# Eight pair sums per band go from VectorE to accumulating transfers begun by GpSimd, and a grouped convolution is placed in nine steps of TensorE's order

## Chip, cores and metric

The kernel runs on one core of a Trainium2 chip. The metric is the device time of one execution in microseconds (us), as the median of several executions. The engines are called PE (TensorE), DVE (VectorE), ACT (ScalarE), POOL (GpSimd) and SP (SyncE).

## What is computed

The input is x of shape (8, 128, 128, 128): images, channels, rows, columns, in float32. There are two stages. The first, `mix_tokens`, is windowed attention and a two-layer perceptron; the change doesn't touch it. The second, `convolve`, is this, cut from the reference:

```
enh  = conv3x3_depthwise(conv1x1(x))                       # 128 channels
h    = conv3x3(x, groups=16)                               # 16 channels
attn = conv1x1(h1 * h2) * gamma + conv1x1(x)               # 16 coefficients for each pixel; h1, h2 are the halves of h
attk = einsum('bpn,nm->bpm', attn, selfw)                  # for each pixel: 64 groups x 2 outputs x (2 channels x 9 taps)
y    = sum over channel of the pair and tap of attk * shifted enh, plus attn @ selfb
out  = y * ga1 + enh + x
```

## The kernel before

An image is cut into 8 bands of 16 rows, so there are 64 bands. Every engine runs its own instruction list through `pipelined(engine, bands, 4, step)`: one step handles up to four bands at once, `l, m, n, o` (the newest first), each in another part of the work. In a step the heavy part is that of band `n`: 36 products, numbered q = 0 to 35. q stands for chunk j = q // 9 (4 rows, 512 pixels, one PSUM bank) and tap t = q % 9.

For product q, PE makes the kernels of both channel halves with two matmuls (`basis_kernels`, L826, into `ps_k`, two buffers of two banks). DVE multiplies them with the shifted `enh` (`product`, L1055) into `products`, a ring of 12 buffers of 128 x 1024. PE then adds a product up by transposing it into `ps_t` (`add_term`, L842, eight 128 x 128 transposes that accumulate). After the last term of a chunk come four transposes of `enh_x`, which is enh + x (L850), ACT copies the sum to SBUF (L946), and PE transposes it back and adds the bias term (`back`, L857 and L859).

To spare PE a third of the terms, twelve pairs (q, q + 1) are summed before they reach it. Eight pairs, `VECTOR_MERGES`, are summed by DVE (L1062) and four, `POOL_MERGES` = 6, 15, 24, 33, by POOL (L765). That leaves 24 terms.

The order on each engine is written out by hand:

- PE goes through 36 slots a step. In slot q it issues the kernels of product q + 2, which wait until product q is made; then the terms whose `TERM_SLOT` is q or, for band `o`, q + 36; then `back`; then pairs of grouped-convolution matmuls (`group_taps`, L809, 18 pairs a band) whose entry in `CONV_SLOTS` is this slot, or this slot + 36; then `coefficients` (L816, slot 22) and a pointwise block (L795, `PW_SLOTS`). A matmul of the grouped convolution fills 32 of 128 columns of PE; a pair of entries covers two chunks in two column groups.
- POOL goes through 16 places a step: 16 additions of a depthwise tap that ACT has scaled (`add_tap`, L753; eight on 10 rows, eight on 8 rows, at places 0 to 7 and 8 to 15), `add_input` (L758, place 1.5, which waits for the last chunk sum of the band before), and the four merges at places 2.6, 5.5, 10.5 and 13.95. All are executed in the order of their places.
- DVE goes through q = 0 to 35: the product, then the merge of q - 2 if there is one. It also does its part of `add_input` (L1046), `h_prod` (L1079) and `att_lo` (L1082).
- SP issues all transfers of the stage: bands in, chunks out, the swap of channel pairs in `enh`, and the coefficient rows.

Buffer reuse is guarded in `buffer_free`: product q may overwrite buffer q % 12 once the term or the merge that read it is done.

Of the kernel before, what the change touches and what calls it, by code (L numbers as in the profile page):

```python
# [44 lines left out]
TAPS = 9  # L45
# [4 lines left out]
HALVES = ((0, 10), (10, 18))  # L50


VECTOR_MERGES = (0, 3, 10, 12, 18, 21, 27, 30)
POOL_MERGES = (6, 15, 24, 33)

OPS = [op for q in range(Q) for op in [("product", q)] + [("merge", q - 2)] * (q - 2 in VECTOR_MERGES)]
OP_COUNT = {op: i + 1 for i, op in enumerate(OPS)}
PARTNERS = {q + 1 for q in VECTOR_MERGES + POOL_MERGES}

TERMS = [q for q in range(Q) if q not in PARTNERS]  # L60
VECTOR_TERMS = [q for q in TERMS if q not in POOL_MERGES]
TERM_SLOT = dict(zip(TERMS, (3, 4, 8, 9, 13, 11, 11, 16, 18, 19, 21, 19, 22, 24, 25, 26, 30, 28, 31, 33, 35, 36, 40, 37)))
FIRST_TERM = [min((TERM_SLOT[q], q) for q in TERMS if q // TAPS == j)[1] for j in range(CHUNKS)]
LAST_TERM = [max((TERM_SLOT[q], q) for q in TERMS if q // TAPS == j)[1] for j in range(CHUNKS)]
TERM_COUNT = {q: i + 1 for i, q in enumerate(sorted(VECTOR_TERMS, key=lambda q: (TERM_SLOT[q], q)))}

BACK_SLOTS = [15, 23, 32, 42]

POOL_PLACES = 2 * (TAPS - 1)
ADD_INPUT_PLACE = 1.5  # L70
# [8 lines left out]

H_PROD_SLOT = 21  # L80
ATT_HIGH, ATT_LOW = 23.8, 25
CONV_SLOTS = [28, 28, 29, 31, 34, 34, 37, 37, 38, 39, 42, 43, 43, 46, 46, 48, 48, 50]
COEFFICIENT_SLOT = 22
PW_SLOTS = [13, 17, 20, 24, 27]

# [445 lines left out]
def convolve(nc, x2, out, w_pw, b_pw, w_dw, b_dw, w_g, b_g, w_att, b_att, w_211, b_211, gamma, ga1, selfb, selfw):  # L531
# [4 lines left out]
    with ExitStack() as ctx:  # L536
# [64 lines left out]
        tap_ready, dw_done, enh_ready, enh_x_ready = sem("tap_ready"), sem("dw_done"), sem("enh_ready"), [sem(f"enh_x_ready{i}") for i in range(2)]  # L601
        swapped = [[sem(f"swapped{p}_{h}") for h in range(2)] for p in range(2)]
        k_done, product_ready, term_done = sem("k_done"), sem("product_ready"), sem("term_done")
        pool_merged, pool_term_done = sem("pool_merged"), sem("pool_term_done")
        sum_done, sumT_ready, back_done, out_ready = sem("sum_done"), sem("sumT_ready"), sem("back_done"), sem("out_ready")
        stored = [sem(f"chunk_stored{j}") for j in range(CHUNKS)]
# [18 lines left out]
        with nc.Block() as block:  # L625
# [87 lines left out]
            def _(pool):  # L713
# [46 lines left out]

                def merge(n, index):
                    q = POOL_MERGES[index]
                    pool.wait_ge(product_ready, len(OPS) * n + OP_COUNT["product", q + 1])
                    lead = products[:, q % PRODUCTS, :, :]
                    nc.gpsimd.tensor_tensor(lead, lead, products[:, (q + 1) % PRODUCTS, :, :], ALU.add).then_inc(pool_merged, 1)  # L765


                ORDER = ([(t - 1, add_tap, 1, (0, t)) for t in range(1, TAPS)] +
                         [(TAPS - 1 + t - 1, add_tap, 1, (1, t)) for t in range(1, TAPS)] +
                         [(ADD_INPUT_PLACE, add_input, 2, ())] +  # L770
                         [(place, merge, 2, (i,)) for i, place in enumerate(POOL_MERGE_PLACES)])

                def step(items, p):
                    for place, action, part, args in sorted(ORDER, key=lambda entry: entry[0] % POOL_PLACES):
                        k = part + (place >= POOL_PLACES)
                        if items[k] is not None:
                            if action is merge:
# [7 lines left out]
            def _(pe):  # L785
# [32 lines left out]
                def basis_kernels(n, p, q):  # L818

                    j, t = divmod(q, TAPS)  # L820
                    if q >= 2:
                        pe.wait_ge(product_ready, len(OPS) * n + OP_COUNT["product", q - 2])
                    else:
                        at_least(pe, product_ready, len(OPS) * (n - 1) + OP_COUNT["product", q + Q - 2])
                    for s in range(2):
                        mm = nc.tensor.matmul(ps_k[q % 2][:, BANK * s:BANK * (s + 1)], basis[:, 2 * t + s, :], att[p][:, j, :],  # L826
                                              start=True, stop=True)
                    mm.then_inc(k_done, 1)

                def add_term(n, q):  # L830

                    j = q // TAPS
                    if q in POOL_MERGES:
                        pe.wait_ge(pool_merged, len(POOL_MERGES) * n + POOL_MERGES.index(q) + 1)
                    else:
                        kind = "merge" if q in VECTOR_MERGES else "product"
                        pe.wait_ge(product_ready, len(OPS) * n + OP_COUNT[kind, q])
# [62 lines left out]
            def _(act):  # L900
# [53 lines left out]
                def tap_product(m, p, h, t):  # L954

                    dy, dx = divmod(t, 3)
                    lo, hi = HALVES[h]
                    src = e0[p][:, lo + dy:hi + dy, dx:dx + W]
                    if t == 0:
                        if h == 0:  # L960
                            act.wait_ge(e0_ready, PW_CHUNKS * m + PW_CHUNKS)

                            at_least(act, enh_x_ready[0], m - 1)
                            for swap in swapped[p]:
                                at_least(act, swap, rounds(m, p, 32))
                            at_least(act, product_ready, len(OPS) * (m - 1))
# [28 lines left out]
            def _(dve):  # L995
# [35 lines left out]
                def buffer_free(n, q):  # L1031

                    before, at = (n, q - PRODUCTS) if q >= PRODUCTS else (n - 1, q - PRODUCTS + Q)
                    if at in POOL_MERGES:
                        at_least(dve, pool_term_done, len(POOL_MERGES) * before + POOL_MERGES.index(at) + 1)
                    elif at in VECTOR_TERMS:
                        at_least(dve, term_done, len(VECTOR_TERMS) * before + TERM_COUNT[at])
                    elif at - 1 in POOL_MERGES:
                        at_least(dve, pool_merged, len(POOL_MERGES) * before + POOL_MERGES.index(at - 1) + 1)
                    else:  # L1040
                        at_least(dve, product_ready, len(OPS) * before + OP_COUNT["merge", at - 1])

                def add_input(n, p):
                    dve.wait_ge(dw_done, 2 * (TAPS - 1) * (n + 1))
# [11 lines left out]
                                            ps_k[q % 2][:, :].rearrange("c (s h w) -> c s h w", s=2, w=W),  # L1056
                                            enh[p][:, :, r:r + CHUNK_ROWS, dx:dx + W], ALU.mult).then_inc(product_ready, 1)

                def merge(n, q):
                    dve.wait_ge(product_ready, len(OPS) * n + OP_COUNT["product", q + 1])  # L1060
                    lead = products[:, q % PRODUCTS, :, :]
                    nc.vector.tensor_tensor(lead, lead, products[:, (q + 1) % PRODUCTS, :, :], ALU.add).then_inc(product_ready, 1)  # L1062

                def step(items, p):
                    l, m, n, o = items
                    for q in range(Q):
                        if m is not None and q == H_PROD_SLOT:
                            dve.wait_ge(moved, 64 * (m + 1))
                        if n is not None:
# [47 lines left out]
```

## Time and profile before

| | |
|---|---|
| Median of 3 executions | 6324.29 us (6320.84 to 6329.96) |
| The profiled execution | 6323.67 us |
| Its span, first to last instruction | 6321.9 us |
| Mean granted clock of TensorE | 0.993 |
| Busy over the span | PE 94%, PE weight loads 65%, DVE 87%, ACT 55%, POOL 73% |

The busy times are sums over the whole span, and the two stages have different limits, so the second stage, which begins near 2130 us, is looked at in windows of its own. Matmuls are pipelined and their ends are modelled: a busy PE is not PE at its peak, and the distance between the starts of two matmuls says more than their durations.

### The profile page before, as it was taken

To read this page: it belongs to the slowest core of one execution; us is meant where nothing else is said; L and a number is where in the kernel's file an instruction comes from. 1 tells how busy PE (TensorE), PEld (TensorE's weight loads), DVE (VectorE), ACT (ScalarE), POOL (GpSimd) and SP (SyncE) were. 2 spreads that over 40 slices of the span, in tenths; PEclk is the share of its full clock that TensorE was granted. 3 is DMA by queue.
4 is the path that set the end of the run, shared out by engine and by line. 5 is a ranking of instruction groups with operands and counts; after the bars stand their busy time and mean duration, and the time that the engine had idled before them with its cause. 6 is when DMAs were issued, how large, how long until landed. Compare 5 with 4: busy or idle time off the path is not lost.

```text
span 6321.9 us, 117871 instructions
## 1 busy us (share of the span) xinstructions
PE 5944.1 (94%) x39944; PEld 4123.6 (65%) x39944; DVE 5481.4 (87%) x5380; ACT 3446.0 (55%) x4288; POOL 4621.9 (73%) x1893
## 2 busy tenths in 40 slices
PE   8999999999999699999999999999999999999998
PEld 6777777777776366666666666666666666666666
DVE  6777777777776799999999999999999999999999
ACT  6777777777776444444444444444444444444443
POOL 4444444444444698888888888888888888888886
PEclk9999999999999799999999999999999999999999
DMA  2222222222221222211222112222221212112221
GB/s 80 66 66 66 66 66 66 66 66 66 66 66 53 58 67 64 67 60 62 65 63 66 61 60 65 63 66 64 64 62 62 65 62 67 60 61 65 63 66 43
DMA packets 303448, 403.66 MB, mean 64 GB/s; under 512 B 38192, under 2 KB 202736, under 8 KB 303344
## 3 DMA queue, kind: packets, MB, share of 16 engines
q1 hardware_dynamic: 303008, 402.45, 20.3%
q10 hardware_dynamic: 400, 0.69, 0.1%
q8 instruction: 24, 0.39, 0.0%
q14 instruction: 16, 0.13, 0.0%
HBM read 152.26 MB, written 136.31 MB: 46 GB/s over the span
## 4 chain that ended last, share of the span: by engine, by line
PE 49%; issue 9%; DVE 9%; SPq 0%; DVEq 0%; DMA 0%; ACT 0%
PE ps_k L826 16%; PE ps_t L842 16%; PE ps_m L809 9%; DVE products L1055 5%; PE ps_p L795 3%; PE ps_t L859 2%; DVE products L1062 2%; PE ps_t L857 1%; PE ps_t L850 1%; PE ps_m L816 1%; DVE h_prod L1079 1%; DVE products L1021 1%; SPq L631 0%; DVEq L1053 0%; SPq L681 0%
## 5 line engine op out<-in xcount | busy, mean ns | idle before, releaser
L753 POOL TENSOR_TENSOR enh<-enh,tap 128x1280 f32<-128x1280 f32 (+1 forms) x1024 | 2831.9, 2766 | 165.6 <-ACT tap L972 116.7
L1055 DVE TENSOR_TENSOR products<-ps_k,enh 128x1024 f32<-128x1024 f32 x2304 | 2750.6, 1217 | 213.6 <-PE ps_k L826 187.5
L826 PE MATMUL ps_k<-att,basis 128*128 128x512 f32 x4608 | 1764.0, 464 | 197.3 <-DVE products L1055 192.1
L842 PE MATMUL ps_t<-ident,products 128*128 128x128 f32 x12288 | 1568.6, 272 | 0.0
L842 PEld LDWEIGHTS ps_t<-ident,products 128*128 128x128 f32 x12288 | 1426.5, 141 | 184.5
L826 PEld LDWEIGHTS ps_k<-att,basis 128*128 128x128 f32 x4608 | 715.9, 189 | 1089.0 <-DVE products L1055 630.6
L257 POOL TENSOR_TENSOR hidden_lo<-hidden,hidden_hi 128x1024 fp32r<-128x1024 f32 x256 | 651.9, 2565 | 894.2 <-DVE hidden_hi L452 894.2
L972 ACT ACTIVATE tap<-e,dw 128x1280 f32<-128x1280 f32 (+1 forms) x1024 | 1245.8, 1248 | 8.2 <-POOL enh L753 8.2
L1062 DVE TENSOR_TENSOR products<-products 128x1024 f32<-128x1024 f32 x512 | 1110.4, 2169 | 0.0
L765 POOL TENSOR_TENSOR products<-products 128x1024 f32<-128x1024 f32 x256 | 614.8, 2401 | 409.9 <-DVE products L1055 409.9
L809 PE MATMUL ps_m<-xin,gT 128*32 128x512 f32 x4608 | 814.2, 609 | 2.8 <-DVE bias_att L1012 2.8
L946 ACT ACTIVATE summedT<-ps_t 128x512 f32<-128x512 f32 x256 | 153.2, 599 | 1060.3 <-PE ps_t L850 1060.2
L433 ACT ACTIVATE hidden<-ring,bias 128x512 f32<-128x512 f32 x512 | 352.0, 689 | 389.1 <-PE ring L285 387.6
L262 POOL TENSOR_TENSOR x_lo<-xt,x_hi 128x512 fp32r<-128x512 f32 x256 | 321.0, 1277 | 183.6 <-DVE x_hi L469 183.6
L282 PE MATMUL ring<-x_hi,w_hi 128*128 128x512 f32 x1024 | 426.9, 417 | 6.6 <-DVE x_hi L469 2.6
L285 PE MATMUL ring<-x_lo,w_hi 128*128 128x512 f32 x1024 | 432.5, 422 | 0.4 <-POOL x_lo L262 0.4
L920 ACT ACTIVATE e<-ps_p,bias_pw 128x512 f32<-128x512 f32 (+1 forms) x320 | 192.7, 602 | 412.6 <-PE ps_p L795 412.6
L283 PE MATMUL ring<-x_hi,w_lo 128*128 128x512 f32 x1024 | 406.7, 397 | 0.0
L795 PE MATMUL ps_p<-xin,pwT 128*128 128x512 f32 x640 | 334.6, 605 | 14.1 <-DMA xin<-layer_out 8.5
L456 DVE TENSOR_REDUCE row_sum<-expd 128x8 f32<-128x512 f32 x128 | 87.8, 686 | 295.3 <-ACT expd L409 295.3
L951 ACT ACTIVATE out_sb<-ps_t 128x512 f32<-128x512 f32 x256 | 152.7, 596 | 325.3 <-PE ps_t L859 325.3
L285 PEld LDWEIGHTS ring<-x_lo,w_hi 128*128 128x128 f32 x1024 | 193.0, 188 | 136.9 <-DVE x_lo L489 100.5
(106 smaller groups left out, 7209.7 us busy)
## 6 DMA issues: line engine op xcount, KB each, us to landing
xt<-in_x SPq DMA_DIRECT2D x128, 512.0 KB, 4.1
layer_out<-xo SPq DMA_DIRECT2D x128, 512.0 KB, 2.9
out<-out_sb SPq DMA_DIRECT2D x256, 256.0 KB, 2.0
xin<-layer_out SPq DMA_DIRECT2D x63, 896.0 KB, 5.6
enh<-enh SPq DMA_DIRECT2D x128, 325.0 KB, 2.7
enh<-enh SPq DMA_DIRECT2D x128, 260.0 KB, 2.4
xin<-layer_out SPq DMA_DIRECT2D x63, 384.0 KB, 6.2
att<-att_hi SPq DMA_DIRECT2D x512, 32.0 KB, 1.9
```

The source lines that it names most:

```text
L257: nc.gpsimd.tensor_tensor(hidden_lo[:, h, :, :], hidden[:, h, :, :], hidden_hi[:, h, :, :].bitcast(FP32), ALU.subtract).then_inc(hidden_lo ...
L282: nc.tensor.matmul(out, w_hi[:, w, :], hi, start=start, stop=False)
L285: return nc.tensor.matmul(out, w_hi[:, w, :], lo, start=False, stop=stop)
L753: nc.gpsimd.tensor_tensor(own, own, tap_sb[add % TAP_BUFFERS][:, 0:hi - lo, :], ALU.add).then_inc(dw_done, 1)
L765: nc.gpsimd.tensor_tensor(lead, lead, products[:, (q + 1) % PRODUCTS, :, :], ALU.add).then_inc(pool_merged, 1)
L795: nc.tensor.matmul(ps_p[:, :], pwT[:, :], xin[p][:, CHUNK_ROWS * c:CHUNK_ROWS * (c + 1), 1:W + 1], start=True, stop=True).then_inc(pw_done, 1)
L809: mm = nc.tensor.matmul(ps_m[32 * j:32 * j + 32, :], gT[:, t, :], xin[p][:, r:r + CHUNK_ROWS, dx:dx + W], start=(t == 0), stop=(t == TAPS ...
L826: mm = nc.tensor.matmul(ps_k[q % 2][:, BANK * s:BANK * (s + 1)], basis[:, 2 * t + s, :], att[p][:, j, :], start=True, stop=True)
L842: mm = nc.tensor.matmul(ps_t[j % 2][:, C * r:C * (r + 1)], products[:, q % PRODUCTS, s, C * r:C * (r + 1)], ident[:, :], is_transpose=True ...
L972: nc.scalar.activation(tap_sb[add % TAP_BUFFERS][:, 0:hi - lo, :], src, ACT.Copy, scale=dw[:, t:t + 1]).then_inc(tap_ready, 1)
L1055: nc.vector.tensor_tensor(products[:, q % PRODUCTS, :, :].rearrange("c s (h w) -> c s h w", w=W), ps_k[q % 2][:, :].rearrange("c (s h w) - ...
L1062: nc.vector.tensor_tensor(lead, lead, products[:, (q + 1) % PRODUCTS, :, :], ALU.add).then_inc(product_ready, 1)
```

## The change

DVE no longer sums pairs. For each of the eight pairs (now 0, 3, 9, 12, 18, 21, 27, 30; 9 in the place of 10), POOL waits for product q + 1 and begins a transfer of 128 x 1024 float32 from SBUF to SBUF that adds the partner's buffer to the lead's. PE waits for the landing, on a semaphore of its own for each pair, before it takes the term. The transfers get places in POOL's order by a formula: (q + 2.5) / 36 x 16, which is 1.11, 2.44, 5.11, 6.44, 9.11, 10.44, 13.11 and 14.44. `TERM_SLOT` is written anew, so that such a term comes 5.5 slots behind the place; the slots of the four POOL merges' terms stay (13, 21, 30, 40). `CONV_SLOTS` holds each slot twice, nine different slots in place of twelve. The counters of `product_ready` now count products alone (Q = 36 a band).

```diff
-VECTOR_MERGES = (0, 3, 10, 12, 18, 21, 27, 30)
+DMA_MERGES = (0, 3, 9, 12, 18, 21, 27, 30)
 POOL_MERGES = (6, 15, 24, 33)
-OPS = [op for q in range(Q) for op in [("product", q)] + [("merge", q - 2)] * (q - 2 in VECTOR_MERGES)]
-TERM_SLOT = dict(zip(TERMS, (3, 4, 8, 9, 13, 11, 11, 16, 18, 19, 21, 19, 22, 24, 25, 26, 30, 28, 31, 33, 35, 36, 40, 37)))
+TERM_SLOT = {0: 8, 2: 4, 3: 11, 5: 9, 6: 13, 8: 10,
+             9: 17, 11: 14, 12: 20, 14: 16, 15: 21, 17: 19,
+             18: 26, 20: 23, 21: 29, 23: 25, 24: 30, 26: 28,
+             27: 35, 29: 32, 30: 38, 32: 34, 33: 40, 35: 37}
...
+DMA_MERGE_PLACES = {q: (q + 2.5) / Q * 2 * (TAPS - 1) for q in DMA_MERGES}
...
-CONV_SLOTS = [28, 28, 29, 31, 34, 34, 37, 37, 38, 39, 42, 43, 43, 46, 46, 48, 48, 50]
+CONV_SLOTS = [28, 28, 31, 31, 33, 33, 36, 36, 39, 39, 42, 42, 44, 44, 47, 47, 50, 50]
...
+        dma_merged = {q: sem(f"dma_merged{q}") for q in DMA_MERGES}
...
+                def merge_by_dma(n, q):
+                    pool.wait_ge(product_ready, Q * n + q + 2)
+                    pool.sem_inc(dma_merge_begun, 1)
+                    nc.gpsimd.dma_start(products[:, q % PRODUCTS, :, :], products[:, (q + 1) % PRODUCTS, :, :],
+                                        accum_op=ALU.add).then_inc(dma_merged[q], 16)
...
-                         [(place, merge, 2, (i,)) for i, place in enumerate(POOL_MERGE_PLACES)])
+                         [(place, merge, 2, (i,)) for i, place in enumerate(POOL_MERGE_PLACES)] +
+                         [(place, merge_by_dma, 2, (q,)) for q, place in DMA_MERGE_PLACES.items()])
...
+                    elif q in DMA_MERGES:
+                        pe.wait_ge(dma_merged[q], 16 * n + 16)
...
-                def merge(n, q):
-                    dve.wait_ge(product_ready, len(OPS) * n + OP_COUNT["product", q + 1])
-                    lead = products[:, q % PRODUCTS, :, :]
-                    nc.vector.tensor_tensor(lead, lead, products[:, (q + 1) % PRODUCTS, :, :], ALU.add).then_inc(product_ready, 1)
...
-                            if ("merge", q - 2) in OPS:
-                                merge(n, q - 2)
```

## Rows read from the trace of the kernel before

**Rows 1.** The page, parts 1 and 2: busy time, and DVE in 40 slices.

```profile
PE 5944.1 (94%) x39944; PEld 4123.6 (65%) x39944; DVE 5481.4 (87%) x5380; ACT 3446.0 (55%) x4288; POOL 4621.9 (73%) x1893
...
DVE  6777777777776799999999999999999999999999
```

**Rows 2.** Window: length, busy us of PE, PEld, DVE, ACT, POOL, clock, DMA share, GB/s.

```profile
3000.00:6000.00 3000.00, 2865.91 (x17586) 1888.00 (x17583) 2851.91 (x2154) 1439.82 (x1696) 2610.22 (x962) 1.00 0.20 63
```

**Rows 3.** The instruction att_lo, 3000 to 6000 us: count, durations, first and last start.

```profile
L1082 DVE SCALAR_TENSOR_TENSOR att_lo<-ps_m,bias_att,att_hi x46: 731/735/737, 3038.8 to 5985.5; 128x512 fp32r<-128x512 f32 x46
```

**Rows 4.** Waits, 3000 to 6000 us: us in total, times, longest us.

```profile
PE ps_k L826 <- DVE products L1055: 134.1, 183, 1.7
```

**Rows 5.** Groups by line, 3000 to 6000 us: count, busy us, mean ns, idle before.

```profile
L753 POOL TENSOR_TENSOR enh<-enh,tap 128x1280 f32<-128x1280 f32 (+1 forms) x733 | 2030.5, 2770 | 91.3 <-ACT tap L972 59.0
L1055 DVE TENSOR_TENSOR products<-ps_k,enh 128x1024 f32<-128x1024 f32 x1649 | 1970.1, 1217 | 147.4 <-PE ps_k L826 129.7
...
L1062 DVE TENSOR_TENSOR products<-products 128x1024 f32<-128x1024 f32 x367 | 804.2, 2191 | 0.0
...
L765 POOL TENSOR_TENSOR products<-products 128x1024 f32<-128x1024 f32 x183 | 438.9, 2399 | 271.3 <-DVE products L1055 271.3
...
L758 POOL TENSOR_TENSOR enh_x<-enh,xin 128x1536 f32<-128x1536 f32 x46 | 155.2, 3374 | 22.9 <-PE ps_t L850 22.9
```

**Rows 6.** Timeline of DVE and POOL in one band: start us, us.

```profile
4032.35 1.22 DVE L1062 TENSOR_TENSOR products<-products 128x1024 f32<-128x1024 f32 x1
...
4040.99 1.23 DVE L1055 TENSOR_TENSOR products<-ps_k,enh 128x1024 f32<-128x1024 f32 x1 [0.21 <-PE ps_k L826]
...
4074.63 3.61 DVE L1062 TENSOR_TENSOR products<-products 128x1024 f32<-128x1024 f32 x1
...
4023.46 4.47 POOL L753 TENSOR_TENSOR enh<-enh,tap 128x1024 f32<-128x1024 f32 x2
...
4036.80 2.40 POOL L765 TENSOR_TENSOR products<-products 128x1024 f32<-128x1024 f32 x1 [5.73 <-DVE products L1055]
...
4071.68 5.48 POOL L753 TENSOR_TENSOR enh<-enh,tap 128x1280 f32<-128x1280 f32 x2
```

**Rows 7.** Timeline of PE in the same band: start us, us.

```profile
4021.41 1.02 PE L795 MATMUL ps_p<-xin,pwT 128*128 128x512 f32 x2
...
4022.73 1.04 PE L842 MATMUL ps_t<-ident,products 128*128 128x128 f32 x8
4023.52 0.72 PE L826 MATMUL ps_k<-att,basis 128*128 128x512 f32 x2
4024.08 1.03 PE L842 MATMUL ps_t<-ident,products 128*128 128x128 f32 x8
...
4027.72 1.07 PE L809 MATMUL ps_m<-xin,gT 128*32 128x512 f32 x8
4028.72 0.72 PE L826 MATMUL ps_k<-att,basis 128*128 128x512 f32 x2
4029.37 1.05 PE L809 MATMUL ps_m<-xin,gT 128*32 128x512 f32 x4
4030.36 0.73 PE L826 MATMUL ps_k<-att,basis 128*128 128x512 f32 x2
...
4040.15 0.71 PE L826 MATMUL ps_k<-att,basis 128*128 128x512 f32 x2
```

**Rows 8.** Timeline of SP, the issues of eight small transfers.

```profile
4019.88 5.04 SPq L681 DMA_DIRECT2D att<-att_hi  x8
```

**Rows 9.** DMA issues, page part 6: count, KB each, us to landing.

```profile
xt<-in_x SPq DMA_DIRECT2D x128, 512.0 KB, 4.1
layer_out<-xo SPq DMA_DIRECT2D x128, 512.0 KB, 2.9
...
xin<-layer_out SPq DMA_DIRECT2D x63, 896.0 KB, 5.6
```

More of the change, by code:

```diff
@@ L50 @@
 HALVES = ((0, 10), (10, 18))
-VECTOR_MERGES = (0, 3, 10, 12, 18, 21, 27, 30)
+DMA_MERGES = (0, 3, 9, 12, 18, 21, 27, 30)
 POOL_MERGES = (6, 15, 24, 33)
-OPS = [op for q in range(Q) for op in [("product", q)] + [("merge", q - 2)] * (q - 2 in VECTOR_MERGES)]
-OP_COUNT = {op: i + 1 for i, op in enumerate(OPS)}
-PARTNERS = {q + 1 for q in VECTOR_MERGES + POOL_MERGES}
+MERGES = DMA_MERGES + POOL_MERGES
+PARTNERS = {q + 1 for q in MERGES}
 TERMS = [q for q in range(Q) if q not in PARTNERS]
-VECTOR_TERMS = [q for q in TERMS if q not in POOL_MERGES]
-TERM_SLOT = dict(zip(TERMS, (3, 4, 8, 9, 13, 11, 11, 16, 18, 19, 21, 19, 22, 24, 25, 26, 30, 28, 31, 33, 35, 36, 40, 37)))
+LONE_TERMS = [q for q in TERMS if q not in POOL_MERGES]
+TERM_SLOT = {0: 8, 2: 4, 3: 11, 5: 9, 6: 13, 8: 10,
[3 rows of a table added]
 FIRST_TERM = [min((TERM_SLOT[q], q) for q in TERMS if q // TAPS == j)[1] for j in range(CHUNKS)]
 LAST_TERM = [max((TERM_SLOT[q], q) for q in TERMS if q // TAPS == j)[1] for j in range(CHUNKS)]
-TERM_COUNT = {q: i + 1 for i, q in enumerate(sorted(VECTOR_TERMS, key=lambda q: (TERM_SLOT[q], q)))}
+TERM_COUNT = {q: i + 1 for i, q in enumerate(sorted(LONE_TERMS, key=lambda q: (TERM_SLOT[q], q)))}
 BACK_SLOTS = [15, 23, 32, 42]
+DMA_MERGE_PLACES = {q: (q + 2.5) / Q * 2 * (TAPS - 1) for q in DMA_MERGES}
 POOL_PLACES = 2 * (TAPS - 1)
@@ L603, in convolve @@
         k_done, product_ready, term_done = sem("k_done"), sem("product_ready"), sem("term_done")
+        dma_merge_begun = sem("dma_merge_begun")
+        dma_merged = {q: sem(f"dma_merged{q}") for q in DMA_MERGES}
         pool_merged, pool_term_done = sem("pool_merged"), sem("pool_term_done")
@@ L762, in merge @@
                     q = POOL_MERGES[index]
-                    pool.wait_ge(product_ready, len(OPS) * n + OP_COUNT["product", q + 1])
+                    pool.wait_ge(product_ready, Q * n + q + 2)
                     lead = products[:, q % PRODUCTS, :, :]
                     nc.gpsimd.tensor_tensor(lead, lead, products[:, (q + 1) % PRODUCTS, :, :], ALU.add).then_inc(pool_merged, 1)
+                def merge_by_dma(n, q):
+                    pool.wait_ge(product_ready, Q * n + q + 2)
+                    pool.sem_inc(dma_merge_begun, 1)
+                    nc.gpsimd.dma_start(products[:, q % PRODUCTS, :, :], products[:, (q + 1) % PRODUCTS, :, :],
+                                        accum_op=ALU.add).then_inc(dma_merged[q], 16)
                 ORDER = ([(t - 1, add_tap, 1, (0, t)) for t in range(1, TAPS)] +
@@ L776, in step @@
                         if items[k] is not None:
-                            if action is merge:
+                            if action in (merge, merge_by_dma):
                                 action(items[k], *args)
@@ L821, in basis_kernels @@
                     if q >= 2:
-                        pe.wait_ge(product_ready, len(OPS) * n + OP_COUNT["product", q - 2])
+                        pe.wait_ge(product_ready, Q * n + q - 1)
                     else:
-                        at_least(pe, product_ready, len(OPS) * (n - 1) + OP_COUNT["product", q + Q - 2])
+                        at_least(pe, product_ready, Q * n + q - 1)
                     for s in range(2):
@@ L834, in add_term @@
                         pe.wait_ge(pool_merged, len(POOL_MERGES) * n + POOL_MERGES.index(q) + 1)
-                    else:
-                        kind = "merge" if q in VECTOR_MERGES else "product"
-                        pe.wait_ge(product_ready, len(OPS) * n + OP_COUNT[kind, q])
+                    elif q in DMA_MERGES:
+                        pe.wait_ge(dma_merged[q], 16 * n + 16)
+                    else:
+                        pe.wait_ge(product_ready, Q * n + q + 1)
                     if q == FIRST_TERM[j]:
@@ L965, in tap_product @@
                                 at_least(act, swap, rounds(m, p, 32))
-                            at_least(act, product_ready, len(OPS) * (m - 1))
+                            at_least(act, product_ready, Q * (m - 1))
                         nc.scalar.activation(enh[p][:, 0, lo:hi, 1:W + 1], src, ACT.Identity, bias=bias_dw[:, 0:1],
@@ L1035, in buffer_free @@
                         at_least(dve, pool_term_done, len(POOL_MERGES) * before + POOL_MERGES.index(at) + 1)
-                    elif at in VECTOR_TERMS:
-                        at_least(dve, term_done, len(VECTOR_TERMS) * before + TERM_COUNT[at])
+                    elif at in LONE_TERMS:
+                        at_least(dve, term_done, len(LONE_TERMS) * before + TERM_COUNT[at])
                     elif at - 1 in POOL_MERGES:
@@ L1040, in buffer_free @@
                     else:
-                        at_least(dve, product_ready, len(OPS) * before + OP_COUNT["merge", at - 1])
+                        at_least(dve, dma_merged[at - 1], 16 * before + 16)
                 def add_input(n, p):
```

## The prediction

> **What bounds the kernel now.** I begin with engine shares and slices [rows 1]. No engine is full over the whole span, and VectorE (DVE) and GpSimd (POOL) step up where the second stage begins, so the stage is read alone. From 3000 to 6000 us [rows 2] TensorE (PE) is busy 2866 of 3000 us (96%), DVE 2852 (95%), POOL 2610 (87%), at clock 1.00, which is the 2.4 GHz level; so no time is lost to the clock. The step of one band is read from an instruction that comes once in it: att_lo, 46 times between starts at 3038.8 and 5985.5 us [rows 3], so 2946.7 / 45 = 65.5 us a band. There are 64 bands: a microsecond saved in each is 64 us of the span.
>
> Who makes the band 65.5 us long? By the waits [rows 4] PE stands idle for DVE's products 134 us in 45.8 bands, 2.9 us a band; DVE for PE 130 us, 2.8 [rows 5]. Neither is clearly the limit: products and kernels alternate over two PSUM buffers, PE is slightly the longer, and where DVE adds a pair PE runs dry. POOL has room: its merges wait for products 271 us [rows 5], 5.9 us a band, nearly all at one of them (5.73 at 4036.80 [rows 6]).
>
> **What goes from DVE.** The eight L1062 sums take 804 us in 45.8 bands [rows 5], 17.5 us a band. Alone such a sum takes 1.22 us (at 4032.35, POOL idle until 4036.80); beside POOL's adds 3.61 us (at 4074.63) [rows 6]. DVE's rest is 62.3 - 17.5 = 45 us (62.3 is 95% of 65.5). It stops being a limit. POOL's adds have the same quarrel: ten rows take 2.70 us in the pair at 4071.68 (next start 2.78 later), eight rows 2.20 in the pair at 4023.46 (4.47 less the pause of 0.08, halved) [rows 6], against the mean of 2.77 for both sizes [rows 5]. POOL's own work becomes 8 x 2.78 + 8 x 2.28 + 4 x 2.37 (L765) + 3.35 (L758) = 53.3 us, down from 57.
>
> The Trainium skill ("SBUF — State Buffer", Who interferes with whom) states that a VectorE instruction with two SBUF inputs and a GpSimd one that reads SBUF take turns on a shared port, and one with a single SBUF input does not. By that rule, the trace agrees: L1062 varies threefold, while L1055, which reads PSUM and SBUF, is steady at 1.22 us.
>
> **What goes from PE.** The grouped convolution goes from 12 places to 9. A place with four column groups (4027.72) takes 1.00 us until the next ps_k, one with two groups (4029.37) 0.99 [rows 7]: filling a half-empty place is free. A ps_k pair ahead of a place takes 0.65 (from 4028.72) instead of 0.56 (from 4023.52), so each place removed gives 1.1 us, 3.3 a band. The 24 terms stay. PE's floor is 65.5 - 2.9 - 3.3 = 59.3 us. Were that all, the gain would be 6.2 us a band, 400 us.
>
> **What comes to POOL, and its order.** Eight transfers of 512 KB a band. No row shows an accumulating transfer or one begun by GpSimd, so two prices are bounded: D, the time POOL is held by one, and L, from there to landing. For D the nearest row is SP's pace, 8 issues in 5.04 us, 0.63 each [rows 8]; above, the POOL add of the same shape, 2.40 [rows 5]. An accumulating row names three places instead of two, so I take 1.5 times SP's, D = 0.95. For L: transfers of 512 KB land 2.9 and 4.1 us after issue, 896 KB 5.6 us [rows 9]. An accumulating one moves three streams of 512 KB (two read, one written) instead of two, so 1.5 times 2.9 to 1.5 times 4.1, 4.4 to 6.2 us; I take L = 5.2. Its ends are 2.9 (the second read is free) and 8.2 (twice 4.1).
>
> In the place of DVE's sums, each transfer has 5.5 of 36 slots, 5.5 x 65.5 / 36 = 10 us, between its place and its term. But POOL executes in order, and two of them stand behind a POOL merge that waits for a later product. merge 15 (place 5.5) waits for product 16; behind it tap 7, then transfer 12 (place 6.44), whose term PE wants in slot 20. merge 33 (13.95) waits for product 34; behind it tap 7 of the lower half, then transfer 30 (14.44), wanted in slot 38, which is slot 2 of the next step. PE is in order as well: everything behind that term, the kernels for the coming products too, stands.
>
> PE from slot 20's term until the kernels of product 34 (slot 32), costed by [rows 7]: 8 terms each with a ps_k pair at 1.34 (4022.73 to 4024.08), 4 pairs alone at 0.55, two places 2.2, three pointwise blocks at 0.77 (4021.41 to 4022.73, less a pair), the coefficients, of the same shape, 0.8, one back 0.6 (half a term and one matmul), two enh_x sums 0.8 (each half a term): 19.6 us. From slot 2 to the kernels of product 16: the same terms and pairs 12.9, four places 4.4, one pointwise 0.8, back 0.6, enh_x 0.8: 19.5. After each the product still needs 1.6 us (DVE starts at 4040.99 [rows 6], 0.84 after its pair at 4040.15, of which 0.55 is counted; 1.2 for itself; 0.1 to reach POOL). The cycle through both is 19.6 + 19.5 + 2 x 1.6 + merges 2 x 2.4 + taps 2.8 + 2.3 + 2(D + L) = 52.2 + 2(D + L).
>
> The half after product 34 is longer than that, as POOL comes late to merge 15. add_input (L758) waits for the last sum of the band before, which PE makes in slot 4, behind the term of transfer 30. From product 34: merge and tap 4.65, D + L, PE's slots 2 to 4 up to that sum (terms 30 and 33 at 0.8, two ps_k pairs at 0.55, one place 1.1, enh_x 0.4) 4.2; then POOL's add_input 3.35, tap 2.8, transfer D, merge 6 2.4, three taps 8.3, transfer D: 16.8 + 2D; merge 15 and tap 5.2, D + L, and 19.6 + 1.6 to the next product 34. Sum: 52.1 + 4D + 2L. With my values 52.1 + 3.8 + 10.4 = 66.3 us, and the first cycle is 52.2 + 12.3 = 64.5.
>
> So the band takes the longest of PE's 59.3, POOL's 53.3 + 8 x 0.95 = 60.9, 64.5 and 66.3 us: 66.3, 0.8 more than now: 64 x 0.8 = 51 us. The sum is made against the profiled execution, 6323.7 us (span 6321.9, 1.8 around it), within 0.6 of the median of 6324.3. Forecast: 6324 + 51 = 6375 us. PE waits more than before though it does less; the saved 17.5 us on DVE turn into idle time. The stages before are untouched.
>
> **Rivals.**
>
> 1. Forecast (chance 0.49): the two late transfers set the band, slower; 65.7 to 70.7 us (D = 1.4 and L = 6.5: 52.1 + 5.6 + 13.0), that is 6337 to 6657 us.
> 2. The same cycle, but transfers land fast (0.36), the other side. It needs 4D + 2L below 13.4; with D = 0.95, L below 4.8. For it speaks the 2.9 us row; against it that this row is a plain copy. At L = 3.5, the middle of the two rows, 52.1 + 3.8 + 7.0 = 62.9 us, 2.6 less: 6158 us. At both lower ends (0.63, 2.9) 60.4 us: 5998.
> 3. GpSimd as the bound (0.10): if D is near the 2.4 of the add it replaces, POOL has 53.3 + 19.2 = 72.5 and the cycle 52.1 + 9.6 + 10.4 = 72.1 us: 72.5, 6772. It decides over the present band from D = 1.5 upward by POOL's sum alone. For it: POOL is the fullest after the change; against it: the rows show issues at 0.63.
> 4. The transfers are hidden (0.05): if POOL does not stand where I put it, PE's 59.3 or POOL's 60.9 decides: 64 x 4.6 less, 6030 us.
>
> The Trainium skill ("DMA: Bandwidth & Descriptors", Anatomy of one DMA) gives a GpSimd-begun transfer 2.0 us plus bytes over 436 GB/s. By that rule an estimate for 512 KB is 3.2 us from issue to landing, on the side of rival 2; no run here shows it for an accumulating one. The same page (Specifications) puts the first byte at about 1 us for transfers begun by GpSimd against 0.6 from SP; the trace agrees with SP's side only as far as its issue pace of 0.63 goes.
>
> **From this to the numbers.** No change, within 0.2% (about 13 us, what a measurement of this kernel can tell), is the strip between cases 1 and 2 (4D + 2L within 0.2 of 13.4): 0.09, of it 0.05 from case 1 and 0.04 from rival 2. Faster: 0.32 of rival 2 and 0.05 of rival 4, 0.37. Slower: 0.44 of case 1 and 0.10 of rival 3, 0.54. The range reaches from the point of rival 2, 6158, to the end of case 1, 6657 us; beyond each end lies about 1 in 10. Case 1's own range is 6337 to 6657.
>
> **What would show it.** In the profile after: L1062 gone, DVE near 68% (45 of 66.3) of the stage; L753 steady at 2.7 and 2.2; POOL's transfers with their D; in the waits, PE's terms idle for the transfers twice a band (slots 20 and 2), not eight times; POOL idle at add_input for PE's enh_x sum. Wrong would be: transfers that land within 4 us (then faster), one that holds POOL for over 1.5 us, waits at all eight terms (then transfers share the DMA engines badly: they are busy 20% now [rows 2], and 64 x 8 x 512 KB are 268 MB on top), or a band set by PE with no idle time.

## The result, and the profile after

The changed kernel takes 6977.7 us (median of 4, 6967.6 to 6991.0); the kernel before took 6325.9 us in the same comparison. The ratio is 1.103, 95% interval 1.101 to 1.106: slower by 10%, outside the range of 6158 to 6657 us. The direction is the forecast one, the size is not: 51 us were forecast and 652 came. The profiled execution took 6967.6 us, with a span of 6965.8 us.

The page, its parts 1, 2 and 3, against [rows 1]:

```profile
PE 5921.9 (85%) x39944; PEld 4206.8 (60%) x39944; DVE 5002.3 (72%) x4868; ACT 3429.3 (49%) x4288; POOL 4725.3 (68%) x2405
...
PEclk9999999999988998998999999899999899999989
DMA  2111111112123444444444444444444444444444
...
q0 software_dynamic: 73728, 268.47, 20.3%
```

The first stage, up to about 2130 us, is as before. In the second every compute engine is less busy than before, the DMA engines are more than twice as busy (the transfers are queue q0, 268 MB), and the granted clock, which was full, is not. The window from 3500 to 6500 us answers to [rows 2], the occurrences of att_lo to [rows 3] (count, durations in ns, first and last start):

```profile
3500.00:6500.00 3000.00, 2465.11 (x15222) 1682.67 (x15220) 2172.15 (x1547) 1235.54 (x1464) 2324.56 (x1151) 0.92 0.47 110
```

```profile
L1087 DVE SCALAR_TENSOR_TENSOR att_lo<-ps_m,bias_att,att_hi x39: 741/742/743, 3559.7 to 6433.0; 128x512 fp32r<-128x512 f32 x39
```

A band takes (6433.0 - 3559.7) / 38 = 75.6 us instead of 65.5. 64 bands of 10.1 us more are 646 us, nearly the whole loss of 652. Who waits, from 3500 to 6500 us (us in total, times, longest), against [rows 4]:

```profile
PE ps_k L837 <- DVE products L1067: 374.4, 40, 9.4
...
PE ps_t L854 <- DMA products<-products: 156.6, 118, 1.6
```

In 39.7 bands PE waits for landings 118 times, three a band, 3.9 us. Two a band were foreseen. But it also waits once a band, 40 times, for 9.4 us for a product of DVE, an engine that was to be two thirds busy (68%; it is 72%). The groups on the page name the reason (count, busy us, mean ns):

```profile
L1058 DVE TENSOR_TENSOR enh_x<-enh,xin 128x512 f32<-128x512 f32 x64 | 615.7, 9621 | 0.0
...
L775 POOL DMA_DIRECT2D products<-products x512 | 472.4, 923 | 7.8 <-DVE products L1067 7.8
```

L1058 is DVE's part of `add_input`, 128 x 512 with both operands in SBUF. The change doesn't touch it. It takes 9.6 us in the mean. The timeline of one band (start us, us; first DVE, then POOL, then PE):

```profile
4499.26 1.22 DVE L1067 TENSOR_TENSOR products<-ps_k,enh 128x1024 f32<-128x1024 f32 x1 [1.34 <-PE ps_k L837]
4500.40 9.83 DVE L1058 TENSOR_TENSOR enh_x<-enh,xin 128x512 f32<-128x512 f32 x1
```

```profile
4497.36 0.86 POOL L775 DMA_DIRECT2D products<-products  x1
4497.97 3.23 POOL L762 TENSOR_TENSOR enh_x<-enh,xin 128x1536 f32<-128x1536 f32 x1
4500.87 2.97 POOL L757 TENSOR_TENSOR enh<-enh,tap 128x1280 f32<-128x1280 f32 x1
```

```profile
4503.50 1.17 POOL L775 DMA_DIRECT2D products<-products  x1
4504.11 2.94 POOL L769 TENSOR_TENSOR products<-products 128x1024 f32<-128x1024 f32 x1
4506.42 9.12 POOL L757 TENSOR_TENSOR enh<-enh,tap 128x1280 f32<-128x1280 f32 x3
```

```profile
4501.30 0.74 PE L837 MATMUL ps_k<-att,basis 128*128 128x512 f32 x2
4511.42 1.22 PE L837 MATMUL ps_k<-att,basis 128*128 128x512 f32 x2 [9.38 <-DVE products L1067]
4512.44 1.91 PE L854 MATMUL ps_t<-ident,products 128*128 128x128 f32 x8
```

L1058 starts while POOL does its own part of `add_input` and ends in the middle of the last POOL row, behind the first of its three taps. POOL goes through add_input, tap, transfer, merge, tap without a gap; each starts before the one ahead of it ends (4500.87 against 4497.97 + 3.23 = 4501.20). Behind the first of the three taps comes the first pause, 0.07 to 0.08 us as between any two taps, and there DVE gets in. DVE stands until then, and the products with it, and so PE. When PE goes on, its transposes run at half speed: eight take 1.91 us where they took 1.04 [rows 7]. That is the 1.2 GHz level, after 9.4 us in which PE did nothing.

In the kernel before the same instruction stood beside the same two additions of POOL (one DVE row, then two of POOL):

```profile
4053.31 1.15 DVE L1046 TENSOR_TENSOR enh_x<-enh,xin 128x512 f32<-128x512 f32 x1
```

```profile
4050.53 3.38 POOL L758 TENSOR_TENSOR enh_x<-enh,xin 128x1536 f32<-128x1536 f32 x1 [0.49 <-PE ps_t L850]
4053.88 3.16 POOL L753 TENSOR_TENSOR enh<-enh,tap 128x1280 f32<-128x1280 f32 x1
```

There it was let in when POOL's add_input ended at 4053.91, though the tap had begun 0.03 us earlier. In the changed kernel add_input stands behind a transfer; it begins before that one's end and hands an overlap of 0.33 us on.

### The profile page after: what moved, and what is told of

Its sections match the earlier page's. It is cut to its first block, busy times and chain, and to the rows that moved or that the text cites. A ratio compares the mean times of both kernels' runs of the same rounds, so it can differ in the third digit from the quotient of the medians.

```text
span 6965.8 us, 117933 instructions
## 1 busy us (share of the span) xinstructions
PE 5921.9 (85%) x39944; PEld 4206.8 (60%) x39944; DVE 5002.3 (72%) x4868; ACT 3429.3 (49%) x4288; POOL 4725.3 (68%) x2405
## 4 chain that ended last, share of the span: by engine, by line
issue 32%; POOL 19%; PE 8%; DMA 6%; ACT 3%; DVE 1%; POOLq 1%; SPq 1%; ACTq 0%; DVEq 0%
POOL enh L757 13%; DMA products<-products 6%; POOL products L769 4%; PE ps_t L854 4%; POOL products L775 2%; ACT tap L984 2%; PE ps_k L837 2%; PE ps_p L806 1%; PE ps_t L862 1%; DVE products L1033 0%; PE ps_m L820 0%; SPq L635 0%; PE ps_t L871 0%; ACT enh L952 0%; POOLq L754 0%
## 5 line engine op out<-in xcount | busy, mean ns | idle before, releaser
L1067 DVE TENSOR_TENSOR products<-ps_k,enh 128x1024 f32<-128x1024 f32 x2304 | 2794.8, 1223 | 1330.6 <-PE ps_k L837 1291.8
L757 POOL TENSOR_TENSOR enh<-enh,tap 128x1280 f32<-128x1280 f32 (+1 forms) x1024 | 2679.1, 2616 | 260.0 <-ACT tap L984 221.5
L854 PE MATMUL ps_t<-ident,products 128*128 128x128 f32 x12288 | 1678.7, 282 | 257.4 <-DMA products<-products 257.4
L854 PEld LDWEIGHTS ps_t<-ident,products 128*128 128x128 f32 x12288 | 1490.8, 146 | 529.1 <-DMA products<-products 340.5
L837 PEld LDWEIGHTS ps_k<-att,basis 128*128 128x128 f32 x4608 | 763.2, 196 | 1378.2 <-DVE products L1067 857.9
L769 POOL TENSOR_TENSOR products<-products 128x1024 f32<-128x1024 f32 x256 | 679.5, 2654 | 872.2 <-DVE products L1067 872.2
L820 PE MATMUL ps_m<-xin,gT 128*32 128x512 f32 x4608 | 656.7, 645 | 2.7 <-DVE bias_att L1024 2.7
L1058 DVE TENSOR_TENSOR enh_x<-enh,xin 128x512 f32<-128x512 f32 x64 | 615.7, 9621 | 0.0
L775 POOL DMA_DIRECT2D products<-products x512 | 472.4, 923 | 7.8 <-DVE products L1067 7.8
L806 PE MATMUL ps_p<-xin,pwT 128*128 128x512 f32 x640 | 360.2, 647 | 16.2 <-DMA xin<-layer_out 10.5
```

What stands on the lines that cost most here:

```text
L757: nc.gpsimd.tensor_tensor(own, own, tap_sb[add % TAP_BUFFERS][:, 0:hi - lo, :], ALU.add).then_inc(dw_done, 1)
L775: nc.gpsimd.dma_start(products[:, q % PRODUCTS, :, :], products[:, (q + 1) % PRODUCTS, :, :], accum_op=ALU.add).then_inc(dma_merged[q], 16)
L806: nc.tensor.matmul(ps_p[:, :], pwT[:, :], xin[p][:, CHUNK_ROWS * c:CHUNK_ROWS * (c + 1), 1:W + 1], start=True, stop=True).then_inc(pw_done, 1)
L820: mm = nc.tensor.matmul(ps_m[32 * j:32 * j + 32, :], gT[:, t, :], xin[p][:, r:r + CHUNK_ROWS, dx:dx + W], start=(t == 0), stop=(t == TAPS ...
L1058: nc.vector.tensor_tensor(enh_x[:, ADD_SPLIT:ROWS, :], enh[p][:, 0, ADD_SPLIT + 1:ROWS + 1, 1:W + 1], xin[p][:, ADD_SPLIT + 2:ROWS + 2, 1: ...
L1067: nc.vector.tensor_tensor(products[:, q % PRODUCTS, :, :].rearrange("c s (h w) -> c s h w", w=W), ps_k[q % 2][:, :].rearrange("c (s h w) - ...
```

## The experiments

All are compared with the kernel before on the same chip. The period of a band is read from att_lo as above, between 3000 and 6300 us.

### DVE's part of add_input at another moment

```diff
-VECTOR_ADD_SLOT = 8
+VECTOR_ADD_SLOT = 15
```

> The changed kernel with DVE's part of add_input (L1058) moved from slot 8 to slot 15, a moment in which POOL stands idle. Theory A, one blocked DVE instruction makes the loss: L1058 took 9.80 us in the changed kernel against 1.15 before, and PE, which gets no products meanwhile, falls to the lower clock behind it. Then L1058 is under 2 us here and the band falls from 75.6 us by 8.6 for it and about 1 for the clock, to 66 us; the execution is 6968 - 64 x 9.6 = 6350 us, within 60. Theory B, the transfers and POOL's order hold the band by themselves and the blocked instruction lies beside them: L1058 is short as well, but the band stays above 71 us and the time above 6680 us.

Measured: 6922.5 us, ratio 1.095 (1.093 to 1.097). L1058 fell to 1.9 us, as both theories said, but the time hardly moved. Theory B seemed to win. A wait of this kernel, 3500 to 6300 us, shows why that reading is wrong:

```profile
PE ps_p L806 <- DMA xin<-layer_out: 279.7, 37, 8.0
```

A new wait of 7.6 us a band took the place of the old one: SP loads the second part of a coming band's rows only when DVE's `add_input` has read the buffer, and PE's first pointwise block in slot 13 needs them. The experiment moved two things. It decides nothing.

### A pause behind POOL's add_input

```diff
                                             xin[p][:, 2:ADD_SPLIT + 2, 1:W + 1], ALU.add).then_inc(enh_x_ready[0], 1)
+                    pool.wait_ge(enh_x_ready[0], n + 1)
```

> The changed kernel with one added wait on POOL: after its part of add_input it waits for that addition's own semaphore before the next tap, which makes a pause of about 0.08 us as between two taps. L1058 stays in slot 8. Theory P, DVE's instruction with two SBUF inputs gets its turn only where POOL pauses between two instructions: L1058 ends right after POOL's add_input, in 1.3 to 2 us, and the band is as in the run with slot 15, 66 us (6350 us). Rival, something else keeps DVE out from the transfer's issue on (the descriptors being written, or the landing): L1058 stays above 5 us and the time above 6600 us.

Measured: 6505.1 us, ratio 1.028 (1.027 to 1.030). One added wait of POOL gives back 473 us of the 652. Two rows of POOL's timeline, then L1059 (the same instruction as L1058, one line lower) and att_lo from 3000 to 6000 us:

```profile
4477.48 3.20 POOL L762 TENSOR_TENSOR enh_x<-enh,xin 128x1536 f32<-128x1536 f32 x1
4480.91 2.89 POOL L757 TENSOR_TENSOR enh<-enh,tap 128x1280 f32<-128x1280 f32 x1 [0.24 <-POOL enh_x L762]
```

```profile
L1059 DVE TENSOR_TENSOR enh_x<-enh,xin x44: 1286/1334/1367, 3046.4 to 5990.6; 128x512 f32<-128x512 f32 x44
L1088 DVE SCALAR_TENSOR_TENSOR att_lo<-ps_m,bias_att,att_hi x44: 741/742/743, 3013.7 to 5958.0; 128x512 fp32r<-128x512 f32 x44
```

With 0.24 us between the two POOL instructions DVE is let in: 1.33 us. The blocked instruction was the main cause. But the band is 2944.3 / 43 = 68.5 us, not the 66 that were expected. One band of this kernel shows PE's four waits for a landing, the terms of transfers 3, 12, 18 and 30 in this order:

```profile
4491.04 1.97 PE L855 MATMUL ps_t<-ident,products 128*128 128x128 f32 x8 [2.67 <-DMA products<-products]
...
4510.67 1.83 PE L855 MATMUL ps_t<-ident,products 128*128 128x128 f32 x8 [1.58 <-DMA products<-products]
...
4524.05 1.09 PE L855 MATMUL ps_t<-ident,products 128*128 128x128 f32 x8 [1.51 <-DMA products<-products]
...
4544.71 1.09 PE L855 MATMUL ps_t<-ident,products 128*128 128x128 f32 x8 [1.07 <-DMA products<-products]
```

Transfers 12 and 30 are the two that the prediction named. Transfer 18 is begun late, as POOL stands for a tap of ACT ahead of it, and transfer 3 is slow: it is begun 1.9 us behind SP's load of a coming band's rows, which the end of POOL's `add_input` releases, and lands 7.3 us after its issue, where transfers 12 and 30 take 4.5. In order of time, SP's load, transfer 3 and the tap ahead of transfer 18:

```profile
4481.81 1.29 SPq L670 DMA_DIRECT2D xin<-layer_out  x2
4483.74 0.88 POOL L776 DMA_DIRECT2D products<-products  x1
4516.13 2.20 POOL L757 TENSOR_TENSOR enh<-enh,tap 128x1024 f32<-128x1024 f32 x1 [3.86 <-ACT tap L985]
```

### What hands the overlap on: transfer 0, transfer 3, or none

Three kernels leave transfers out; the partners' products are then missing from the sums, and PE takes the lead product alone. With `LEFT_OUT = (0,)`, `(3,)` or all eight:

```diff
-                         [(place, merge_by_dma, 2, (q,)) for q, place in DMA_MERGE_PLACES.items()])
+                         [(place, merge_by_dma, 2, (q,)) for q, place in DMA_MERGE_PLACES.items() if q not in LEFT_OUT])
...
-                    elif q in DMA_MERGES:
+                    elif q in DMA_MERGES and q not in LEFT_OUT:
...
-                    else:
+                    elif at - 1 not in LEFT_OUT:
```

> The changed kernel with transfer 0 alone left out, the one that POOL begins just ahead of its add_input (its partner is missing from the sum). In the changed kernel POOL's instructions overlap by 0.3 us behind a transfer and by 0.6 behind a second one, with no gap in which DVE's L1058 gets in. If the overlap that add_input inherits from transfer 0 is what blocks, L1058 is let in at the end of add_input as in the kernel before, 1.2 to 2 us, and the time is near that with the pause, 6500 us. If any transfer or merge behind it blocks, L1058 stays above 5 us and the time above 6850 us.

> The changed kernel with transfer 3 alone left out, the one that POOL begins while L1058 stands blocked (its partner is missing from the sum). If the overlap inherited from transfer 0 blocks, L1058 is still shut out through add_input, the tap and merge 6, above 7 us. If the transfer that comes while it waits is to blame, L1058 gets in at an earlier boundary, under 5 us.

> The changed kernel with all eight transfers left out: POOL doesn't begin them, PE takes the lead product alone as the term, so the eight partners are missing from the sums. No pause added, L1058 in slot 8. It prices the transfers and tests what blocks DVE. If L1058 is blocked by transfers among POOL's additions, it is back at 1.2 us here; if back-to-back additions on POOL are enough, it stays above 5 us. If it is short, the band is PE's own: my floor was 59.3 us, so 6324 - 64 x 6.2 = 5930 us; if above 62 us a band (6100), the floor in the prediction was too low.

Without transfer 0: 6579.0 us (one execution), DVE's `add_input`, L1059 here, at 1.05. Without transfer 3: 6923.4 us (one execution), still shut out. POOL and DVE in the kernel without transfer 0, then DVE's `add_input` in the one without transfer 3:

```profile
4320.72 2.94 POOL L763 TENSOR_TENSOR enh_x<-enh,xin 128x1536 f32<-128x1536 f32 x1 [0.54 <-PE ps_t L863]
4323.61 3.16 POOL L758 TENSOR_TENSOR enh<-enh,tap 128x1280 f32<-128x1280 f32 x1
```

```profile
4323.16 1.05 DVE L1059 TENSOR_TENSOR enh_x<-enh,xin 128x512 f32<-128x512 f32 x1
```

```profile
L1059 DVE TENSOR_TENSOR enh_x<-enh,xin x40: 8852/8928/8982, 3053.6 to 5975.8; 128x512 f32<-128x512 f32 x40
```

It is the transfer in front of `add_input` that does it, not the one that is begun while DVE stands. Here the overlap at 4323.61 is 0.05 us, as before the change, and DVE gets in; transfer 3 behind it, at 4326.71, doesn't shut it out. (That transfer again lands late, 7.2 us after its issue, with SP's load begun at 4324.72 and transfer 0 not there at all.) Why this kernel takes 74 us more than the one with the pause was not tested by a run; from 3000 to 6000 us PE stands 6.9 us a band for landings instead of 6.5, and its granted clock is 0.96 instead of 0.98.

With no transfers: 5935.0 us, ratio 0.938 (0.937 to 0.940), and a band of (5863.4 - 3015.4) / 48 = 59.3 us:

```profile
L1088 DVE SCALAR_TENSOR_TENSOR att_lo<-ps_m,bias_att,att_hi x49: 737/743/744, 3015.4 to 5863.4; 128x512 fp32r<-128x512 f32 x49
```

This is the floor of PE that the prediction had worked out, 59.3 us.

### The order of transfer 0 and add_input

```diff
-DMA_MERGE_PLACES = {q: (q + 2.5) / Q * 2 * (TAPS - 1) for q in DMA_MERGES}
+DMA_MERGE_PLACES = {q: (q + 2.5) / Q * 2 * (TAPS - 1) for q in DMA_MERGES} | {0: 1.6}
```

> The changed kernel with one step of POOL's order changed: add_input stands ahead of transfer 0 and not behind it (place of transfer 0: 1.6). No pause is added, all eight transfers are made. Theory, add_input begun before the transfer in front of it is over carries an overlap of 0.3 us with it that shuts DVE out: add_input is now begun behind a tap, with an overlap of 0.04 us, L1058 is let in at its end, 1.0 to 1.4 us, and the time is near that of the pause, 6450 to 6600 us. Rival, the pause helped for another reason and any transfer near L1058 shuts it out: L1058 above 5 us, the time above 6850 us.

Measured: 6677.6 us, ratio 1.057 (1.055 to 1.058). POOL, then DVE:

```profile
4497.43 2.94 POOL L762 TENSOR_TENSOR enh_x<-enh,xin 128x1536 f32<-128x1536 f32 x1 [0.54 <-PE ps_t L862]
4500.30 0.86 POOL L775 DMA_DIRECT2D products<-products  x1
```

```profile
4499.87 1.05 DVE L1058 TENSOR_TENSOR enh_x<-enh,xin 128x512 f32<-128x512 f32 x1
```

L1058 takes 1.05 us with all eight transfers made, one of them right behind `add_input`. The theory of the overlap holds. The time is 78 us above the range that I expected: PE stands 8.2 us a band for landings (346.3 us from 3000 to 6000 us) instead of 6.5 with the pause, and its granted clock is 0.96 instead of 0.98. Transfers 0 and 3 are now begun 3.3 us apart, and SP's load of a coming band's rows is issued between them, at 4501.44; transfer 3 lands 10.2 us after its issue. PE's waits for landings, then the time from issue to landing (min/median/max, all transfers, 3500 to 6200 us):

```profile
PE ps_t L854 <- DMA products<-products: 346.3, 170, 4.2
```

```profile
DMA to landing us min/median/max: 4.5/5.6/10.3
```

### The transfers behind merges

On slot 15 (first kernel), and then on the kernel with the pause, transfers 12 and 30 go ahead of merges 15 and 33:

```diff
-DMA_MERGE_PLACES = {q: (q + 2.5) / Q * 2 * (TAPS - 1) for q in DMA_MERGES}
+DMA_MERGE_PLACES = {q: (q + 2.5) / Q * 2 * (TAPS - 1) for q in DMA_MERGES} | {12: 5.4, 30: 13.9}
```

> As the run with slot 15, and transfers 12 and 30 begun ahead of POOL's merges 15 and 33 (places 5.4 and 13.9) instead of behind merge and tap. Prediction's mechanism: each late transfer costs its merge and tap, about 5 us of delay, at PE's slots 20 and 2; with them early those two waits of PE for a landing vanish and the band comes down to PE's floor or POOL's sum, 60 to 62 us: 5.0 us less than with slot 15 alone, about 6030 to 6080 us. Rival: the waits for landings are covered by others (ACT's taps, POOL's arrears), and the gain on the run with slot 15 is under 1 us a band.

Measured: 6812.8 us, ratio 1.078 (1.076 to 1.079), 110 us less than slot 15 alone. The wait for the band's rows is still there (313.0 us in 38 bands, 8.2 each), and the gain is 1.7 us a band instead of 5.0, so this kernel too says little.

> The changed kernel with the pause behind add_input and with transfers 12 and 30 begun ahead of merges 15 and 33; L1058 stays in slot 8, so the load of the next band is not held up as it was with slot 15. The kernel with the pause alone took 6505 us, 68.5 us a band, and PE waits there for landings at four places, 6.5 us a band. Prediction's mechanism: two of the four (slots 20 and 2) come from standing behind a merge and a tap; with them early the band loses 2.6 us of waits seen and up to 2.4 more that they push into the others: 63.5 to 66 us, 6190 to 6350 us. Rival, the transfers are late because POOL is in arrears everywhere: under 1 us a band, above 6440 us.

Measured: 6277.0 us, ratio 0.992 (0.991 to 0.994). The band is (5944.5 - 3032.6) / 45 = 64.7 us, 3.8 less than with the pause alone, in the range expected. PE's waits for landings fall from 157 in 39.4 bands to 83 in 41.7, four a band to two (3500 to 6200 us; the pause alone, then with early transfers, then the two waits that are left in one band, for transfers 3 and 18):

```profile
PE ps_t L855 <- DMA products<-products: 256.3, 157, 2.8
```

```profile
PE ps_t L855 <- DMA products<-products: 142.3, 83, 2.2
```

```profile
4502.65 1.95 PE L855 MATMUL ps_t<-ident,products 128*128 128x128 f32 x8 [1.93 <-DMA products<-products]
...
4530.90 1.09 PE L855 MATMUL ps_t<-ident,products 128*128 128x128 f32 x8 [1.46 <-DMA products<-products]
```

### Later terms for two transfers

```diff
-TERM_SLOT = {0: 8, 2: 4, 3: 11, 5: 9, 6: 13, 8: 10,
+TERM_SLOT = {0: 8, 2: 4, 3: 13, 5: 9, 6: 13, 8: 10,
...
-             18: 26, 20: 23, 21: 29, 23: 25, 24: 30, 26: 28,
+             18: 26, 20: 23, 21: 30, 23: 25, 24: 30, 26: 28,
```

> The kernel with pause and early transfers 12 and 30 (6277 us, 64.6 us a band), and the terms of transfers 3 and 21 taken two slots and one slot later (13 and 30 for 11 and 29). PE stood 1.9 and 1.5 us a band for these two landings. If the landings' latency is what is left between 64.6 and the 59.3 us of the kernel with no transfers, the band loses 2.5 to 3.8 us: 6035 to 6120 us. Rival, the buffers' ring or DVE's order takes the wait over, as a later term frees its buffer later: under 1 us a band, above 6210 us.

Measured: 6139.1 us, ratio 0.971 (0.969 to 0.972), 19 us above the expected range. The band is 62.4 us, 2.3 less. What was expected named the wrong term, though: the wait of 1.46 us ends with the landing of transfer 18 (4525.26 + 5.6 = 4530.86, slot 26), and PE doesn't stand for transfer 21. So the later slot of term 3 has a wait to remove and that of term 21 has none; the two were not tried apart. PE's waits for landings fall to 30.9 us in 43.3 bands (3500 to 6200 us), and its granted clock is 1.00 again. This version beats the kernel before by 2.9%:

```profile
L1088 DVE SCALAR_TENSOR_TENSOR att_lo<-ps_m,bias_att,att_hi x49: 733/735/743, 3001.5 to 5994.6; 128x512 fp32r<-128x512 f32 x49
```

### The nine places by themselves

The nine places on the kernel before, and the twelve old ones on the kernel with pause and early transfers:

```diff
-CONV_SLOTS = [28, 28, 29, 31, 34, 34, 37, 37, 38, 39, 42, 43, 43, 46, 46, 48, 48, 50]
+CONV_SLOTS = [28, 28, 31, 31, 33, 33, 36, 36, 39, 39, 42, 42, 44, 44, 47, 47, 50, 50]
```

> The kernel before with the nine places of the grouped convolution alone (CONV_SLOTS), DVE's sums kept. My sum of the prediction: PE saves 3.3 us a band in places, but DVE is within 3 us of its own floor (62.3 busy of 65.5), so 0.5 to 2.5 us a band are gained: 6164 to 6292 us. If places cost nothing (rival), 6324 us, unchanged; if the new slots bunch PE's work where DVE is ahead, slower than 6330.

> The kernel with pause and early transfers 12 and 30 (6277 us), with the twelve places of the grouped convolution from the kernel before instead of the nine. The prediction priced three places at 3.3 us a band of PE's time; alone, on the kernel before, nine places gave nothing (6319 against 6323 us). If PE's own work counts where DVE no longer sets the pace, it is 3.3 us a band slower, less what fills waits for landings: 6370 to 6490 us. If the place count never matters, 6277 us.

Measured: 6319.4 us on the kernel before, ratio 0.999 (0.998 to 1.000), a gain of 0.2% at most; I had expected at least 32 us, 0.5%. With the twelve places in the other kernel 6476.4 us, ratio 1.024 (1.023 to 1.026), which is 199 us or 3.1 us a band more than with nine. Both readings agree with one cause: while DVE does the sums, PE's saving goes into waiting for DVE (its waits for products rise from 2.9 to 4.7 us a band); once DVE is free, it counts. Not all of the 3.1 us is the price of the places: with twelve PE also stands longer for landings (4.0 us a band against 3.4, 3000 to 6000 us), at a granted clock of 0.98 against 0.99.

## Why the prediction was wrong

**The step that failed** is the one on DVE: "DVE's rest is 62.3 - 17.5 = 45 us [...] It stops being a limit." I left the other DVE instructions at their old durations. DVE's part of `add_input` went from 1.15 to 9.80 us, in a moment when PE has work for two products at most. The pause, transfer 0 left out, and the swapped order each bring it to 1.05 to 1.33 us; leaving transfer 3 out doesn't. The kernel with the pause prices the blocking at 75.6 - 68.5 = 7.1 us a band, 473 us of the 652. I named the rule that two SBUF operands take turns with POOL, and used it only for the sums that the change removes and for POOL's additions beside them, not for the DVE instructions that stay. Of those, the other one with two SBUF operands, h_prod, was not hit: 1.54 us before, 0.88 after.

**The two transfers behind merges** were found right: early, they give 3.8 us a band (5.0 in the expectation of the kernel with slot 15), and of PE's four waits a band with the pause, those two went. So the direction is not luck: without the blocking the kernel is slower by 2.8%, and no longer when these two are early.

**The prices of a transfer** were 0.95 and 5.2 us. Measured, POOL is held 0.92 us in the mean, and a landing comes 4.5 us after the issue begins at the least, 4.6 in the median of the kernel with the pause. So from the end of POOL's part it is about 3.7, below my 5.2. (POOL's next instruction starts 0.6 us after the transfer's start, as far as SP's issues are apart, so even 0.92 is more than the transfer takes out of POOL's order. The prediction also held SP's pace of 0.63 against a first-byte time; a distance between two issues doesn't show one, and no run here does.) With 0.92 and 3.7 my sum 52.1 + 4D + 2L would give 63.2 us, rival 2. The kernel with the pause shows 68.5. So the sum was short by 5.3 us and the price of L too high, and that the 66.3 of the forecast lies near 68.5 is luck.

Two terms were put at nothing. One is the waits for other transfers: I let each land in the same time and gave waits to two. In fact PE waits for four, 6.5 us a band (256.3 in 39.4): also for transfer 3, which lands 7.3 us after its issue beside SP's load, and for transfer 18, ahead of which POOL stands 3.9 us for ACT. The other is the clock. The sum takes it as full, and in the kernel with the pause it is not:

```profile
3000.00:6000.00 3000.00, 2671.60 (x16820) 1812.97 (x16818) 2023.71 (x1711) 1369.09 (x1622) 2563.79 (x1272) 0.98 0.52 122
```

At 0.98 it costs, by an estimate, 2% of 68.5 = 1.4 us a band. Of the 9.2 us between 59.3 and 68.5, the waits for landings and this make 7.9; the rest was not taken apart.

**The floor of PE**, 59.3 us, and within it 3.3 us for three places, came out at 59.3 and 3.1, the latter with longer waits in it. **POOL's additions** were forecast at 2.70 and 2.20 us; from 3500 to 6500 us their means are 2.87 and 2.37, against 3.08 and 2.46 before. They stay above the forecast, as the one behind a transfer reads 0.3 us longer (2.48 against 2.19 for eight rows). Rival 3, POOL as the bound, did not come: POOL is busy 77% of the stage. Rival 4, hidden transfers, is what is left if order and terms are set well, but for 3 us: 62.4 against 59.3.

In one line, a band: 59.3 with no transfers, 62.4 with all in the best order tried, 64.7 with terms 3 and 21 early, 68.5 with transfers 12 and 30 late, 75.6 with DVE shut out.

Open is what in POOL makes the difference between an overlap of 0.03 to 0.07 us, at which DVE is let in (0.07 with the order swapped, 4497.43 + 2.94 against 4500.30), and one of 0.33, at which it is not. The traces show that it goes so, band after band (from 3000 to 6000 us L1058 takes 9.76 to 9.83 us in the changed kernel, and 1.04 to 1.06 with the order swapped), not why; no value in between was tried.

## What to carry to other kernels

Before work is handed to GpSimd, list every DVE instruction with two SBUF operands that remains, and look at what POOL does then: a row of POOL instructions without a gap can hold one back for all of their length, and whatever waits for DVE with it. A pause of 0.24 us between two of them was the cheapest cure here; a transfer begun behind rather than ahead of the addition that DVE overlaps let DVE in as well, but that kernel took 173 us more than the one with the pause. In an engine that works in order, a transfer's place is not its issue time: look for a waiting instruction ahead of it, a merge or an addition that waits for ACT. And look at what other queues start at the same moment: the landing that PE waited for longest was that of the transfer begun beside SP's load.

## What the runs showed of the hardware

- One DVE instruction of 128 x 512 with both operands in SBUF was kept waiting through five POOL instructions, 9.8 us. In the kernel before, such instructions took 3.7 us at the most, their own time of 0.6 to 1.2 us included, so they waited no longer than one POOL instruction takes.
- An accumulating transfer of 512 KB inside SBUF, begun by GpSimd, holds POOL for 0.85 us, and for 1.15 us when it starts itself ahead of its predecessor's end by 0.3 us; either way the instruction behind it starts 0.6 us after its start.
- Such a transfer lands 4.5 us after its issue at the least (transfers 12 and 30 with the pause). Transfers 18 and 21, begun 2.7 us apart, with SP's swap of channels issued 1.3 us ahead of them, took 5.7 and 5.9 us. Transfer 3, begun 1.9 to 2.0 us behind SP's load of 896 and 384 KB, took 7.3 us, and 7.2 us in the kernel without transfer 0, where no other accumulating transfer was near; with transfer 0 begun 3.3 us ahead of it as well it took 10.2 us. So what transfer 3 takes beyond 4.5 us without transfer 0 came beside SP's load and not beside another accumulating transfer; no run left that load out.
- After PE had stood for 9.4 us, its clock was at the 1.2 GHz level for the next instructions (1.91 us for eight transposes), and so it was after 2.67 us (1.97). The length of a wait alone doesn't tell: after 1.58 us for transfer 12 with the pause eight transposes took 1.83 us, after 1.65 us in the kernel without transfer 0 they took 1.09, and after 1.55 us in the changed kernel too.
